# Splitting each row that SyncE fetches from the node table into sixteen pieces of 128 bytes (GINE layers, one core)

## The reference

```python
def _gine_layer(x, src, dst, edge_attr, eps, We, be, W1, b1, gamma, beta, W2, b2):
    e = edge_attr @ We + be
    m = jax.nn.relu(x[src] + e)
    agg = jax.ops.segment_sum(m, dst, num_segments=x.shape[0])
    h = ((1.0 + eps) * x + agg) @ W1 + b1
    mu = jnp.mean(h, axis=0)
    var = jnp.mean(jnp.square(h - mu), axis=0)
    h = (h - mu) * jax.lax.rsqrt(var + BN_EPS) * gamma + beta
    h = jax.nn.relu(h)
    return jax.nn.relu(h @ W2 + b2)
...
for l in range(L):
    x = _gine_layer(x, src, dst, edge_attr, eps[l], We[l], be[l], W1[l], b1[l], gamma[l], beta[l], W2[l], b2[l])
...
x = _layernorm(x + _L0_gnn_ref(x, edge_index, edge_weight1, ...), axis=-1)
```

## Time and profile before

| | us |
|---|---|
| median of three timed runs | 1325.12 |
| lowest, highest | 1322.78, 1325.54 |
| span of the profiled execution | 1599.5 |
| TensorE / VectorE / GpSimd / ScalarE busy in it | 1298.3 / 1034.8 / 817.8 / 521.0 |

### The profile page before, as it was taken

How to read it: one execution, slowest core, us unless ns; L and a number is a source line. 1 busy time by engine, 2 the same in 40 slices (tenths; PEclk the granted TensorE clock), 3 DMA queues, 4 the chain that set the end, 5 groups by cost and what they waited for, 6 DMA issues and landing times.

```text
span 1599.5 us, 24747 instructions
## 1 busy us (share of the span) xinstructions
PE 1298.3 (81%) x7309; PEld 744.8 (47%) x7309; DVE 1034.8 (65%) x2108; ACT 521.0 (33%) x1130; POOL 817.8 (51%) x871
## 2 busy tenths in 40 slices
PE   3537888888896788898796888898797589899887
PEld 3523555544553445554453354555453245455453
DVE  8808667775666766676466666666556666666557
ACT  3532323323262232333252232233244133223224
POOL 0054665555506666666506666666515666666620
PEclk7558999999997899999898799999999799999989
DMA  3254555555637666666636666666636666666633
GB/s 103 81 162 134 169 167 166 157 172 163 185 96 215 174 182 182 175 175 176 176 108 202 173 175 180 176 181 176 169 123 187 179 173 176 181 174 175 182 114 132
DMA packets 93300, 261.78 MB, mean 164 GB/s; under 512 B 19497, under 2 KB 22304, under 8 KB 93162
## 3 DMA queue, kind: packets, MB, share of 16 engines
q0 software_dynamic: 68800, 225.50, 49.7%
q1 hardware_dynamic: 24362, 34.64, 6.7%
HBM read 246.93 MB, written 12.94 MB: 162 GB/s over the span
## 4 chain that ended last, share of the span: by engine, by line
PE 66%; issue 10%; another core or an unknown queue 9%; DVE 7%; DMA 3%; SPq 3%; ACT 2%; ACTq 0%; DVEq 0%
PE y_ps L1860 22%; PE pair_ps L1813 18%; PE h_ps L1938 9%; PE y_ps L1983 6%; DMA src_onehot<-near_ws 2%; PE uT_ps L1891 2%; PE uT_ps L1898 2%; PE uT_ps L1884 2%; SPq L672 2%; DVE rows L1422 1%; DVE rows L1333 1%; PE uT_ps L1873 1%; ACT rows L948 1%; DVE src_onehot L1269 1%
## 5 line engine op out<-in xcount | busy, mean ns | idle before, releaser
L771 POOL DMA_INDIRECT rows<-node_table,src_fast x860 | 815.1, 948 | 717.1 <-issue 300.7
L1422 DVE SCALAR_TENSOR_TENSOR rows<-We_ps,negw_fast,rows 128x512 f32<-128x512 f32 x860 | 591.6, 745 | 22.4 <-DMA rows<-node_table,src_fast 15.8
L1860 PE MATMUL y_ps<-table_parts,src_onehot 128*128 128x512 f32 x1520 | 459.1, 432 | 140.9 <-issue 82.8
L1860 PEld LDWEIGHTS y_ps<-table_parts,src_onehot 128*128 128x128 f32 x1520 | 276.3, 198 | 439.7 <-issue 343.6
L948 ACT ACTIVATE rows<-y_ps 128x512 f32<-128x512 f32 x380 | 221.1, 602 | 614.1 <-remote 302.9
L1813 PE MATMUL pair_ps<-rows,onehot 128*32 128x512 f32 x2504 | 391.5, 646 | 24.2 <-issue 18.8
L1269 DVE TENSOR_TENSOR src_onehot<-y_ps,src_bc 126x256 fp32r<-126x256 f32 x352 | 144.6, 420 | 163.9 <-remote 85.3
L1938 PE MATMUL h_ps<-uT,W_sb 128*128 128x128 f32 x1152 | 149.2, 283 | 46.8 <-issue 46.5
L1938 PEld LDWEIGHTS h_ps<-uT,W_sb 128*128 128x128 f32 x1152 | 140.5, 196 | 64.4 <-issue 62.1
L1813 PEld LDWEIGHTS pair_ps<-rows,onehot 128*32 128x32 f32 x2504 | 60.8, 112 | 150.3 <-issue 138.6
L1983 PE MATMUL y_ps<-rows,hT 128*128 128x512 f32 x288 | 124.5, 593 | 0.0
(11 more groups left out here) (239 smaller groups left out, 823.5 us busy)
## 6 DMA issues: line engine op xcount, KB each, us to landing
late_rows<-node_table SPq DMA_DIRECT2D x1536, 2.0 KB
rows<-node_table,src_fast POOLq DMA_INDIRECT x860
node_table<-rows SPq DMA_DIRECT2D x29, 256.0 KB
src_onehot<-near_ws SPq DMA_DIRECT2D x380, 2.0 KB
x_now<-x_pad SPq DMA_DIRECT2D x10, 512.0 KB, 7.5
W_sb<-W SPq DMA_DIRECT2D x4, 1024.0 KB, 5.4
rows<-W SPq DMA_DIRECT2D x16, 256.0 KB
out<-rows SPq DMA_DIRECT2D x8, 256.0 KB
```

Of the source, the lines that this page charges most:

```text
L771: nc.gpsimd.indirect_dma_start(rows[:, slot, :], None, table[:, :], bass.IndirectOffsetOnAxis(src_fast[:, t:t + 1], 0)).then_inc(landed[q] ...
L1422: last = nc.vector.scalar_tensor_tensor(rows[:, slot, :], We_ps[:, :], negw_fast[:, t:t + 1], row, ALU.mult, ALU.max)
L1860: last = nc.tensor.matmul(y_ps[k % 2][:, :], src_onehot[:, 2 * (k % ONEHOTS) + b, :], table_parts[:, part, 2 * pair_of(k) + b, :], start=( ...
```

## The change

`late_rows` gets, for every tile, sixteen shares of 32 numbers with one number of padding behind each, and the DMA of a row names sixteen pieces of 128 bytes on both sides. The padding keeps the sixteen from being one run of bytes in SBUF. VectorE reads the three tiles through a three-dimensional view that skips the padding, and writes and reads its other operands in the same shape. Nothing is added to any engine's program, and nothing in it moves: on SyncE the DMAs at L672 read 1x16x128 bytes where they read 1x2048, and on VectorE three instructions a layer have other shapes.

```diff
+    ROW_SHARES = 16
+    SHARE = D // ROW_SHARES
...
-        late_rows = sb("late_rows", [P, len(ROW_TILES), D])
+        late_rows = sb("late_rows", [P, len(ROW_TILES), ROW_SHARES, SHARE + 1])
...
-                    sp.dma_start(late_rows[p:p + 1, m, :].bitcast(u8),
-                                 table_bytes[:, bass.ds(place_of, ROW_BYTES)]).then_inc(rows_landed[m], 16)
+                    sp.dma_start(late_rows[p:p + 1, m, :, 0:SHARE].bitcast(u8),
+                                 table_bytes[:, bass.ds(place_of, ROW_BYTES)].rearrange(
+                                     "o (s b) -> o s b", s=ROW_SHARES)).then_inc(rows_landed[m], 16)
...
+            def by_share(array):
+                return array.rearrange("p (s d) -> p s d", s=ROW_SHARES)
...
                         dve.wait_ge(rows_landed[m], 16 * P * (l + 1))
-                        row = late_rows[:, m, :]
-                    last = nc.vector.scalar_tensor_tensor(rows[:, slot, :], We_ps[:, :], negw_fast[:, t:t + 1], row,
-                                                          ALU.mult, ALU.max)
+                        last = nc.vector.scalar_tensor_tensor(
+                            by_share(row), by_share(We_ps[:, :]), negw_fast[:, t:t + 1], late_rows[:, m, :, 0:SHARE],
+                            ALU.mult, ALU.max)
+                    else:
+                        last = nc.vector.scalar_tensor_tensor(row, We_ps[:, :], negw_fast[:, t:t + 1], row,
+                                                              ALU.mult, ALU.max)
```

## The result

The changed kernel takes **1710.05 us** (median of 4 runs, 1709.54 to 1714.3) against 1324.36 us before in the same series: a ratio of 1.292, 95% interval 1.290 to 1.294. It is slower by 386 us, 96 us a layer.

What follows compares the result with a forecast made beforehand. It took TensorE as busiest (66% of the chain) and SyncE as nearly full but not the bound. Longer turns less the lead, 68 us, plus 12 make 80 a layer, 320 in four: 1325 + 320 = 1645 us, range 1322 to 1745.

Steps and rivals of the forecast that it cites:

- nothing happens: Rival on SyncE: the issue costs 0.10 us or less and rows are prefetch; 1323 to 1328 us, chance 0.13.
- longer turns: SyncE's 85 turns a layer become 3.76 us against 2.72, 1.04 too long: 88 us a layer.
- the lead: SyncE's weights are issued ahead of TensorE's tile; taken off once a layer: 20 us.
- the rows behind the last weights: The 11 groups on SyncE after a layer's last weights: 44 rows x 0.363 = 16, less 4: 12 us a layer.
- the issue decides: Row issue on SyncE, the deciding term: 228 ns becomes 591, +0.363 us a row; forecast chance 0.60.
- The new turn: One weights DMA, one address load and four row DMAs on SyncE: 2.31 + 4 x 0.363 = 3.76 us.
- What SyncE has to spare: SyncE needs 2.31 us of a scaled 2.72 us turn: 0.41 us to spare in each, 15%.
- VectorE's view at 0: Three VectorE instructions a layer through 3-dimensional views: at most 1 us in all, taken as 0.
- DMA engines at 0: 46080 more packets on the DMA engines: upper end 202 us of each, counted 0 while SyncE is slower.
- The signs in the profile: L672's issue 550 to 660 ns, turns 3.8 us or more, SyncE's L658 waits near zero, TensorE about 65% busy, late rows.
- an issue dearer by less: Rival on SyncE: the issue is dearer by 0.15 to 0.25 us; 1335 to 1405 us, chance 0.17.
- the faster case: Rival: one DMA engine carried the rows and gathers wait for it; 1309 us at best, likely 1316, chance 0.10.

Runs made afterwards that it cites:

- before, second profile: The kernel before, unchanged, profiled a second time: 1323.97 us timed, a span of 1322.2 us.
- one more issue: Kernel before with one more DMA of 4 bytes on SyncE ahead of each group of four rows: 1337.61 us, ratio 1.009.
- two more issues: Kernel before with two more DMAs of 4 bytes on SyncE ahead of each group of four rows: 1444.44 us, ratio 1.087.
- sixteen pieces, eight addresses at once: Changed kernel with eight row addresses loaded at once in every second turn: 1655.12 us, ratio 1.245.
- 4.7 tiny issues: Kernel before, rows whole, with 4.7 more 4-byte DMAs on average ahead of each group of four rows: 1727.52 us, ratio 1.306.
- four pieces: Changed kernel with each row cut into four pieces of 512 bytes in place of sixteen of 128: 1829.6 us, ratio 1.380.
- The run with four tiles: Kernel before with SyncE fetching four tiles' whole rows, sixteen addresses loaded at once, eight one-hot buffers in place of ten: 1372.29 us, ratio 1.035.
- the pair of runs with one tile: SyncE fetches only tile 13's rows, GpSimd gathers the other two tiles: rows whole 1335.57 us, rows in sixteen pieces 1334.97 us.

## Why the prediction was right, and where its terms were off

The measured 1710 us lie 65 above the forecast of 1645, inside the forecast's own range (1540 to 1760) and inside the stated one. The stated range, 1322 to 1745, also holds "nothing happens", so lying in it says little. What carries the prediction is its mechanism: the issue went from 228 to 537 ns, and SyncE's turns became the pace of the layer.

**One line through the runs with three tiles.** Let S be the time from the first to the last row DMA that SyncE starts in a layer, the mean of the four layers by the traces, and the layer the distance from one layer's first row to the next's, the mean of three:

| run | S, us | layer, us | layer - S | time, us |
|---|---|---|---|---|
| before, second profile | 228.2 | 304.9 | 76.7 | 1324 |
| one more issue | 246.5 | 308.3 | 61.8 | 1338 |
| two more issues | 275.9 | 335.1 | 59.2 | 1444 |
| sixteen pieces, eight addresses at once | 328.9 | 388.3 | 59.4 | 1655 |
| **sixteen pieces (the change)** | 343.3 | 404.1 | 60.8 | 1710 |
| 4.7 tiny issues | 346.5 | 406.7 | 60.2 | 1728 |
| four pieces | 372.3 | 432.6 | 60.3 | 1830 |

From S = 246 us on, a layer is S + 60 us, whatever SyncE spends S on. Below it, the gathers and TensorE set the 305 us. So the kernel before had 305 - 60 - 228 = 17 us a layer between SyncE's last row and the point where it would be felt, besides its waits inside S, and the change took 115: 98 lost, four times 392 by the line, 386 measured.

The line holds for this interleaving only. The run with four tiles has S = 239 and a layer of 318 us, since no groups of rows stand behind its last weights; there, by the sum in its section, the weights' turns and not the last rows come last.

A rival that the runs settle is TensorE's clock, which fell with the change. In the profiles of the table's last six rows the mean granted clock is 0.949, 0.941, 0.890, 0.879, 0.869 and 0.851, and layer - S stays between 59 and 62 us. The run with tiny issues has the lower clock without any cut. So the clock falls along with the time and adds nothing to the layer that the table could show.

**The sum, term by term.** A layer grew by 404.1 - 304.9 = 99 us in the traces (386 / 4 = 96.5 in timed runs), and the prediction has 80. The terms, by the change and the second profile of before:

| term, us a layer | predicted | in the traces |
|---|---|---|
| longer turns | 85 x (3.76 - 2.72) = 88 | 85 x (3.68 - 2.45) = 105 |
| less the lead | 20 | 17 |
| the rows behind the last weights | 12 | 35.5 - 23.5 = 12 |
| sum | 80 | 100 |

**Point by point.**

- *That the issue decides, and that one partition with several elements is a class of its own with L680 and L648*: right, and what carried the forecast. The size was 537 ns, not 591: 0.22 us less in a turn.
- *The new turn* came to 3.68 us in the mean where I had 3.76 for a smooth one. The cheaper issue is partly eaten by what I had not priced, the weights DMA behind a row DMA of sixteen pieces, 0.16 us; against it, the address loads got shorter, 531 ns for 561. Together 0.08 x 85 = 7 us a layer too dear.
- *What SyncE has to spare* was the step that failed. I took 0.41 us a turn, from 3.29 x 0.828 = 2.72. A layer scaled so came out right (305 us), but a turn did not: its real mean is 2.45 us over the four layers of the second profile, for layer 4 (1217.3 - 1013.1) / 84 = 2.43, of which 2.28 are work. So 0.17 us was spare, as a turn is a smaller part of the layer than the disturbed profile showed. That made the forecast 0.27 x 85 = 23 us a layer too low. It is the largest error; that the turn's price erred the other way by 7 is luck.
- *The lead of 20 us*: right. It was 19.6 to 20.2 us at the last weights of the layers and is 2.1 to 2.8 after the change, so 17 were used up, the same 17 as by the line. The 26 us from which I scaled it were one layer's; the others had 5 to 6.5 us in that profile, so the choice of the long one decided it.
- *The last 11 groups at 12*: right. From the last weights to the last row it is 23.5 us before and 35.5 after. That they are felt shows in VectorE, which waited 76.2 us for rows in four layers, 19 each.
- *VectorE's view at 0*: right, 744 ns against 745. *DMA engines at 0*: right, by the pair of runs with one tile and by the 4.7 tiny issues. The new packets took (0.074 x 1712.5 - 0.080 x 1322.2) = 21 us of each DMA engine's time in the whole run, 7 ns each, where my upper end was 202 us.
- *The signs in the profile*: L674 near 540 ns, turns of 3.6 to 3.7 where I had said 3.8 or more, late rows, as listed. SyncE's waits at L658 were to go to near zero and were 20.1 us, against 46.9 in the second profile. TensorE's busy share did not fall to 65% but to 78%; its busy time includes modelled ends and the lower clock. And the trace puts 437.1 us of the weight loads' waits at L1869 down to issue and not to the DMA of the weights; that these land last is read from the 195 tiles of 340 that begin within 3 us of their issue.
- *The rivals*: an issue dearer by less, and nothing at all, both fell with the 537 ns. By my own sum the price at +0.15 us is 1335 and not the 1350 written there. For the faster case my bound was wrong: I capped it at 16 us from 15.8 us of waits for gathers in the disturbed profile, and in the second profile VectorE waits 165.3 us for them. So no row bounded its price. In the changed kernel it could not show, as the issue was dear; the one-tile pair leaves room for a gain of 7 us at most, for a third of the rows. All the rows spread at a cheap issue was not run.
- *"Nearly full"*, read from SyncE's few waits, came from the same profile. In the second one, its row and weights issues fill 91.2 + 20.8 = 112 of the 228 us of S.

The Trainium skill (Perfetto Trace Analysis, What "DMA-bound" means) names the issuing sequencer as a resource that can bind. The table agrees: a layer is S + 60 us. In the changed kernel the row and weights issues are 209.0 + 34.8 = 244 of the 343 us of S; the rest is address loads, register moves and waits.

## What to carry to other kernels

A queue that issues many small transfers in a fixed order has a period of its own; measure its smooth period and its real mean, and spend no more than the difference unless it is also ahead of what needs it, as the 17 us of lead were here. What a cut of a DMA does to the issuing engine has to be read from issues of the same form: a row cut inside one partition costs the issuer more than twice a whole one, at two pieces as at sixteen. If the span of a profile is a fifth above the timed runs, take a second profile before scaling rates from it: the scaled layer was right, the scaled turn and the waits were not.

## What the runs showed that I had not expected

- The step of 300 ns lies between one piece and two in one partition (252 to 558 ns); from two to 32 pieces the price stays within 100 ns of that; over partitions two pieces cost nothing more (253 ns).
- Four pieces cost the issuer 588 ns in the kernel and sixteen 537, so the finer cut was the faster kernel, 1710 against 1830 us. Why is open.
- A profiled execution of the kernel before was 277 us longer than another of the same program (1599.5 and 1322.2 us), with stalls on SyncE up to 1350 ns. What caused them stays open.
- The granted TensorE clock had a mean of 0.879 in the changed kernel and 0.955 in the second profile of before, in which TensorE is busier (92% against 78%).
